# Which engine multiplies delta*u by B in a selective scan: VectorE, ScalarE, and now GpSimd

## What is computed

```
def step(h, inp):
    u_t, d_t, B_t, C_t = inp
    dA = jnp.exp(d_t[..., None] * A)
    h = dA * h + (d_t * u_t)[..., None] * B_t[:, None, :]
    y = jnp.einsum('bdn,bn->bd', h, C_t)
    return (h, y)
```

## Time and profile before

| | us |
|---|---|
| median of three runs | 911.88 (911.01 to 912.39) |
| the profiled execution's own time | 911.18 |
| its span in the trace | 909.2 |
| scan loop, first pair, steps 3 to 63 (251.8 to 445.6) | 193.8 |
| scan loop, second pair (688.7 to 880.6) | 191.9 |
| mean granted TensorE clock | 0.957 |

### The profile page before, as it was taken

The page is one execution under the profiler, slowest core; times in us unless marked ns, Lnnn a source line. Parts: engine busy times, 40 slices in busy tenths (PEclk is TensorE's granted clock), DMA queues, the critical chain, the costliest instruction groups (busy, mean ns, idle before and its releaser), DMA issues.

```text
span 909.2 us, 10555 instructions
## 1 busy us (share of the span) xinstructions
PE 734.8 (81%) x3866; PEld 499.9 (55%) x3866; DVE 802.6 (88%) x682; ACT 560.2 (62%) x960; POOL 527.1 (58%) x243
## 2 busy tenths in 40 slices
PE   3895999877667788788799889988766677888896
PEld 2342344344466777678655434435446566787783
DVE  6979997769999998999969899775999999989984
ACT  2962242227849898979486723313585987897942
POOL 3105899020479698778510479911127978878851
PEclk9999899999799899999989899999989999999999
DMA  3002000000445455455200120000033455545431
GB/s 113 1 24 69 0 1 0 0 1 0 140 151 174 142 190 191 139 186 179 77 1 0 59 58 0 0 1 0 1 98 120 148 177 173 201 153 182 160 110 23
DMA packets 34065, 78.18 MB, mean 86 GB/s; under 512 B 15704, under 2 KB 15840, under 8 KB 34016
## 3 DMA queue, kind: packets, MB, share of 16 engines
q1 hardware_dynamic: 32608, 76.23, 25.1%
q0 software_dynamic: 320, 1.05, 0.5%
q10 hardware_dynamic: 1088, 0.26, 0.1%
HBM read 70.71 MB, written 2.62 MB: 81 GB/s over the span
## 4 chain that ended last, share of the span: by engine, by line
DVE 35%; PE 29%; ACT 16%; issue 16%; POOL 2%; DMA 0%; DVEq 0%; POOLq 0%; SPq 0%; ACTq 0%
ACT arena L957 13%; PE ps L748 7%; DVE arena L1773 7%; PE ps L509 6%; DVE ps L1764 6%; PE ps L548 4%; DVE HS L1773 3%; DVE arena L1728 3%; PE ps L762 2%; PE ps L640 1%; ACT ps L957 1%; PE ps L662 1%; DVE arena L1748 1%; DVE arena L1667 1%; DVE arena L1646 1%
## 5 line engine op out<-in xcount | busy, mean ns | idle before, releaser
L396 POOL TENSOR_TENSOR arena<-arena 128x1024 f32<-128x1024 f32 x85 | 200.5, 2368 | 59.8 <-DVE arena L1773 54.6
L957 ACT ACTIVATE arena<-arena 128x128 f32<-128x128 f32 (+3 forms) x412 | 157.0, 455 | 86.9 <-DVE arena L1667 67.7
L1773 DVE TENSOR_TENSOR_SCAN arena<-arena,ps 128x1024 f32<-128x1024 f32 x86 | 194.6, 2276 | 9.7 <-ACT arena L957 5.5
L957 ACT ACTIVATE arena<-arena,Amat 128x1024 f32<-128x1024 f32 x128 | 143.0, 1141 | 7.2 <-DVE arena L1773 6.0
L640 PE MATMUL ps<-mat,arena 128*128 128x128 f32 x1016 | 136.6, 279 | 5.6 <-POOL arena L396 5.2
L599 PE MATMUL ps<-mat,arena 128*128 128x128 f32 x560 | 81.6, 294 | 64.4 <-DVE arena L1773 36.9
L640 PEld LDWEIGHTS ps<-mat,arena 128*128 128x128 f32 x1016 | 118.4, 145 | 9.8 <-POOL arena L396 7.9
L748 PE MATMUL ps<-arena,mat 128*128 128x512 f32 x240 | 110.9, 615 | 14.4 <-DVE arena L1643 14.4
L396 POOL TENSOR_TENSOR arena<-HS,arena 128x1024 f32<-128x1024 f32 x42 | 100.1, 2382 | 29.7 <-DVE HS L1773 27.0
L599 PEld LDWEIGHTS ps<-mat,arena 128*128 128x128 f32 x560 | 65.8, 146 | 79.4 <-DVE arena L1773 46.8
L957 ACT ACTIVATE arena<-ps 128x1024 f32<-128x1024 f32 (+2 forms) x55 | 46.1, 849 | 87.2 <-PE ps L486 45.4
(11 more groups left out here) (219 smaller groups left out, 1340.3 us busy)
## 6 DMA issues: line engine op xcount, KB each, us to landing
arena<-c_rows SPq DMA_DIRECT2D x128, 512.0 KB, 3.8
arena<-arena SPq DMA_DIRECT2D x16, 252.0 KB
out<-arena SPq DMA_DIRECT2D x28, 64.0 KB, 2.3
xres<-x POOLq DMA_DIRECT2D x4, 256.0 KB, 5.2
xres<-x SPq DMA_DIRECT2D x4, 256.0 KB, 4.1
convw<-conv_w SPq DMA_DIRECT2D x1, 576.0 KB
c_rows<-ROWS SPq DMA_DIRECT2D x4, 128.0 KB, 1.9
mat<-mats SPq DMA_DIRECT2D x1, 448.0 KB, 3.5
```

What stands on the lines that cost most here:

```text
L396: tt(HC[s % 2], HS[s % 3], CB[s % 4], ALU.mult).then_inc(S("hc"), 1)
L957: return nc.scalar.activation(out_, in_, func, bias=bias, scale=scale, accum_out=accum_out)
L1773: nc.vector.tensor_tensor_scan(HS[s % 3], DA[s % 3], PS[q][:, :], 0.0, ALU.mult, ALU.add).then_inc(S("scan"), 1)
```

## The change

A table of 13 letters, repeated from step 9 to step 62, says who makes the product: Z (DVE), A (ACT in the turned layout), P (POOL in the turned layout). That gives 25 A steps, 8 P steps (14, 20, 27, 33, 40, 46, 53, 59) and 31 Z steps of 64, where there were 29 ACT steps and 35 Z steps. The X steps are then 9, 11, 13, 14, 15, 17, 19, 20, 22, 24, 26, 27, 28, 30, 32, 33, 35, 37, 39, 40, 41, 43, 45, 46, 48, 50, 52, 53, 54, 56, 58, 59, 61.

```
+        ROUTES = "AZAZAPAZAZAPZ"
+        POOL_STEPS = [s for s in range(9, SCANS - 1) if ROUTES[(s - 9) % 13] == "P"]
+        ACT_STEPS = [s for s in range(9, SCANS - 1) if ROUTES[(s - 9) % 13] == "A"]
+        X_STEPS = sorted(ACT_STEPS + POOL_STEPS)
@@ gpsimd
+            def scaled_input(h, s):
+                i, j = X_STEPS.index(s), s // D_STATE
+                pool.wait_ge(S("kept"), max(turned(h, j), 5 * h + ROWS_TURNED))
+                pool.wait_ge(S("bb"), SCANS * h + X_STEPS[i - 3] + 1)
+                parts = 1 if i % 3 < 2 and j % 2 == 0 else 2
+                for part in range(parts):
+                    n, m = part * BLK // parts, BLK // parts
+                    dst = scaled_columns(i, n, m).rearrange("p (k c) -> p k c", c=P)
+                    src = du_columns(j, n, m).rearrange("p (k c) -> p k c", c=P)
+                    last = tt(dst, src, BT[:, n:n + m, j, s % D_STATE].unsqueeze(2).to_broadcast([P, m, P]), ALU.mult)
+                last.then_inc(S("pool_scaled"), 1)
...
                     if not last_step(h, s):
                         state_times_c(h, s)
+                    if s + 5 in POOL_STEPS:
+                        scaled_input(h, s + 5)
@@ tensor, turn_scaled
-                pe.wait_ge(S("scaled"), len(X_STEPS) * h + i + 1)
+                if s in POOL_STEPS:
+                    pe.wait_ge(S("pool_scaled"), len(POOL_STEPS) * h + POOL_STEPS.index(s) + 1)
+                else:
+                    pe.wait_ge(S("scaled"), len(ACT_STEPS) * h + ACT_STEPS.index(s) + 1)
@@ scalar
-                    if s + 3 in X_STEPS:
+                    if s + 3 in ACT_STEPS:
                         scaled_input(h, s + 3)
```

More of the change, by code:

```diff
@@ L173, in fused_blocks @@
         SCANS = 4 * D_STATE
-        X_STEPS = [s for s in range(9, SCANS - 1) if (s % 5 in (0, 2, 4) if 26 <= s < 3 * D_STATE else s % 2 == 1)]
+        ROUTES = "AZAZAPAZAZAPZ"
+        POOL_STEPS = [s for s in range(9, SCANS - 1) if ROUTES[(s - 9) % 13] == "P"]
+        ACT_STEPS = [s for s in range(9, SCANS - 1) if ROUTES[(s - 9) % 13] == "A"]
+        X_STEPS = sorted(ACT_STEPS + POOL_STEPS)
         Z_STEPS = [s for s in range(SCANS) if s not in X_STEPS]
@@ L183, in du_block, with scaled_columns, du_columns @@
             return blk(D[n // 4]["END"], n % 4)
+        def scaled_columns(i, n, m):
+            if i % 3 < 2:
+                return TB[i % 3][:, n * P:(n + m) * P]
+            return D[n // 4]["TB"][:, n % 4 * P:(n % 4 + m) * P]
+        def du_columns(j, n, m):
+            if j % 2 == 0:
+                return D[1]["W4"][:, n * P:(n + m) * P]
+            return D[n // 4]["END"][:, n % 4 * P:(n % 4 + m) * P]
         def turned(h, j):
@@ L1112, in keep_du @@
                 if j >= 2:
-                    act.wait_ge(S("scaled"), len(X_STEPS) * h + sum(1 for s in X_STEPS if s < D_STATE * (j - 1)))
+                    act.wait_ge(S("scaled"), len(ACT_STEPS) * h + sum(1 for s in ACT_STEPS if s < D_STATE * (j - 1)))
+                    act.wait_ge(S("pool_scaled"), len(POOL_STEPS) * h + sum(1 for s in POOL_STEPS if s < D_STATE * (j - 1)))
                 if j == 0:
@@ L1139, in scaled_input @@
                     act.wait_ge(S("bb"), SCANS * h + X_STEPS[i - 3] + 1)
-                if i == 0 or X_STEPS[i - 1] // D_STATE < j:
+                if i == 0 or ACT_STEPS[ACT_STEPS.index(s) - 1] // D_STATE < j:
                     act.wait_ge(S("kept"), turned(h, j) if i else 5 * h + ROWS_TURNED)
```

## The result

The changed kernel takes 918.53 us in the median of four runs (918.25 to 920.44), the kernel before beside it 912.13 (911.01 to 912.44): a ratio of 1.0073, 95% interval 1.0057 to 1.0090. Forecast was 912.4, no change; it is 6 us slower: inside the 902 to 920 that I gave for all cases together, outside the 909 to 916 of the forecast itself, and by another sum than mine. The profiled execution took 918.25 us, its span 916.4, against 911.18 and 909.2.

What follows compares the result with a forecast made beforehand. DVE was taken to bound the scan loops, with POOL following; terms of +1.3 us in the first pair and -0.8 in the second sum to +0.5, giving 912.4 us. Forecast's own range 909 to 916, for all cases 902 to 920.

Steps and rivals of the forecast that it cites:

- the two slow rivals: The cases of a dear POOL product (921 us, chance 0.14) and of POOL's lag in PE's queue (920 us, 0.11).
- the new line: Sign: POOL's new product shows at 2.3 to 2.5 us a set; over 3 us would mean the dear product.
- Steps 3 to 17: First pair: scan 17 later behind ACT's statistics, +1.4 us; second: saved multiply partly waited for C product 11, -0.4.
- Steps 18 to 33, first pair: Two multiplies go, but scan 32 waits 1.3 us for C product 29: -0.8 us.
- Steps 18 to 33, second pair: Two multiplies go, with a wait for C product 29 at scan 32: -1.1 us.
- Steps 34 to 39: Step 34 gains a multiply; PE's chain and ACT's square still set scan 40: +1.2 us in each pair.
- Steps 40 to 49: Step 46's product stands ahead of the root on POOL, so the normalization waits: +2.0 us in each pair.
- the turns on PE: Costed at nothing: as many turns as before, only from another source.
- Steps 50 to 63: Two multiplies go and POOL has room behind scan 49: -2.5 us in each pair.
- The saving comes through: Rival: POOL's products cost DVE nothing, together -9.6 us, so 902.3 us; half of it 907; chance 0.31.
- The product is dear: Rival: POOL's product takes 3.33 us, adding 0.9 at five places per pair, 9 us: 921 us; chance 0.14.
- POOL's lag reaches PE's queue: Rival: late C products hold back PE's fills, 1 us at each of 8 products: 920 us; chance 0.11.

Runs made afterwards that it cites:

- E4: Changed kernel with the same X steps, but all eight POOL products per pair made by ACT, none by POOL; 912.98 us.
- T1: Kernel before, POOL making no product, with steps 37 and 39 turned to Z and 20 and 50 made by ACT; 909.73 us.
- E2: Changed kernel with the root of the variance put ahead of step 46's product on POOL; 912.76 us.
- E5: Changed kernel with eleven matmuls of zeros on PE in its pause ahead of sum 42; 915.66 us.
- E1: Changed kernel with POOL's product cut to one of its eight blocks, order and waits kept, output not right; 907.64 us.
- T3: T2 with POOL making step 24's product too; 911.89 us.
- E2b: As E2, but step 46's product stands behind the C product of step 42 instead of 41; 912.70 us.
- T4: T1 up to step 49, then X steps 50, 52, 54, 56, 58, 61 on ACT and 53, 59 on POOL; 905.94 us.
- T5: T4's X steps, with 53 and 59 made by ACT too and none by POOL; 909.09 us.
- T2: T1 with POOL making the products of steps 56 and 60; 908.87 us.

## Where the prediction held and where it failed

The forecast was no change, the result is 0.7% slower. The 918.5 lie inside 902 to 920 only because the two slow rivals stretched that range, and neither is what happened: that is luck, not a hit. Of the signs that I had named, the normalization's wait (1.73 for 2.0) and scan 40 behind scan 36 came true; the new line took 1.92 and 2.1 us instead of 2.3 to 2.5, POOL was busy for 173 and 172 instead of 178, DVE for 183 and 185 instead of 182, scan 32 didn't wait, and of DVE's gaps, 13.7 and 12.4 us, one is above and one within the 9 to 13 that I called mine. A product cheaper than mine should by my own sum have made the kernel faster, so what I left out is worth more than the 6 us. The steps in turn:

*Steps 3 to 17 (+1.4, -0.4): right.* Measured +0.9 and -0.5. Scan 17 of the first pair waits 1.09 as before, behind the same statistics. The product was 0.4 us shorter than I took it, about the difference.

*Steps 18 to 33, first pair (-0.8): right in size, wrong in the reason.* I wrote that scan 32 would wait for C product 29. It didn't. The time went at scan 26, 1.98 us, for ACT's decay behind step 28's scalings. I had named that row and cost it at next to nothing, since it would "mostly" lie over the same time. E4, without any product on POOL, has the same wait: it belongs to the order of the steps.

*Steps 18 to 33, second pair (-1.1): the step that failed most.* Measured +3.0, 4.1 off. Scan 26 waits here too, 1.79 us, where I had 1.3 for scan 32. Two things are in it that no term had: the delta of 5.38 us instead of 2.64, which is POOL's lateness turned into a longer DVE instruction; and PE's lower clock behind the pause that this makes (4.07 us idle, then turns of 1.9 us), 1.13 at step 21. I followed POOL only for the waits of DVE on POOL's results, and took the lengths of DVE's own instructions as fixed. The trace of before held the sign of the other twice: this delta at 2.50 and 2.64 us where the others took 1.21, and in the earlier trace rows delta*u at 3.33 instead of 2.4, which I used as a bound for a price instead of asking what made it so long.

*Steps 34 to 39 (+1.2): right*, +1.3, and scan 40 11.2 behind the end of scan 36. T1 shows the converse: X steps there save nothing.

*Steps 40 to 49 (+2.0): mechanism right, the sum too small.* The wait for the root was 1.73, and E2 removes just that. But +3.0 and +4.3 were measured, because step 47's multiply waits 1.00 and 2.32 for PE at half its clock. I had cost "the turns on PE" at nothing because there are as many; their number was right and their duration wasn't. E5 gives the term its size: 3.6 us for both. I had put it at nothing without asking whether PE's clock would stay where it was.

*Steps 50 to 63 (-2.5): nearly right*, -2.1; scan 59 waits 0.67 and 0.70 for ACT.

The failed terms add up to 4.1 in the second pair's steps 18 to 33, and 1.0 and 2.3 in steps 40 to 49; the rest 0.6: together 8.0, which is 8.5 less 0.5.

The rivals. *The saving comes through* is false, and E1 shows that up to 13 us, most of them POOL's time, stood against it. *The product is dear* would have given the measured slowing, 921, by a wrong cause: 1.92 us is cheaper than a C product, and the rule of the Trainium skill that I weighed (GPSIMD Engine Reference, Performance pitfalls for Q7 kernels) did not show in an operand that repeats its element: the trace disagrees with the reading of half as much again. *POOL's lag reaches PE's queue* comes nearest: in T3 multiply 26 waits 0.44 and 0.33 us for PE behind one late C product, and step 47 of the changed kernel waited for PE; but its price of 1 us at all eight places is not what happened, and in E5, at full clock, step 47 doesn't wait at all.

Still open is who gets in first when POOL's C products follow one another without a gap. The changed kernel, E2 and E5 gave 5.4 us, E2b 3.08 with the same code up to there, in one profiled execution of each; in all four the delta began 0.36 to 0.38 us behind the first C product's start. E2b's median is the same as E2's, so I don't know how often each occurs. A wait that would keep POOL out of the delta was not tried.

## What to carry to other kernels

Before work is moved to an engine that "has time", list what stands behind it there and is waited for (here one root, 1.7 us a pair), and which instructions of the busy engine can't run beside it (here one delta, up to 2.7 us more): neither shows in busy shares. Look first for the stretch in which the present engine is really the bound: two products on POOL were worth 2 us a pair at the end (T4 against T5), and a single one at step 24 made the pair 2 us longer (T3 against T2; in the first pair half of it was the clock). When the numbers of instructions don't change but an engine's work becomes thinner, check its clock before costing its work at nothing.

## What the runs showed of the hardware

A POOL product whose second operand repeats one element 128 times takes 1.92 us over 128 x 1024, against 2.37 with two full operands.

A DVE addition with both operands in SBUF takes 1.21 us where POOL is idle, and 1.22 where it begins ahead of POOL's instruction (the deltas ahead of the loop). Begun while a POOL instruction ran, it ended 1.08 or 1.09 us behind the end of one in all 28 loops profiled, and took 1.31 to 5.38; where it came in between two of them running, the second took 1.0 us longer (E1, E2b). Scans and multiplies, whose second operand lies in PSUM, took 2.25 to 2.29 and 1.19 to 1.29 us beside POOL throughout. The Trainium skill (SBUF — State Buffer, SBUF: two separate sides) says that the two engines lock a shared pair of ports for a whole instruction and the first to start gets it; these lengths agree. That POOL may hold on to it over two instructions running while DVE waits (5.38), or not (3.08), that sentence does not tell.

PE's granted clock fell to its lower level (1.2 GHz) in stretches of little work: within 4.07 us of idle time in the second pair, and behind the normalization in 8 of 12 loops in the new order, with pauses of 0.86 to 2.87 us before it. Turns of the changed kernel took up to 1.9 us instead of 1.04, and filler products of 2.54 us kept the clock up in both loops of E5. The Trainium skill (TensorE: Matmul & The Clock Gate, The HAM clock gate) has an idle PE fall to half its clock, and the trace agrees in the pause of 4.07 us; behind the normalization PE was not idle but little used, and there the clock fell in some loops and stayed up in others with the same pauses (2.85 us in E2, 2.86 in the changed kernel). What a fall costs here, 1 to 2.3 us, arises on another engine, DVE.
